# Adding three split products in one range of PSUM columns instead of two, in the first layer of a two-layer kernel

## The chip, the cores and the metric

The kernel runs on one core of a Trainium2 chip. The metric is the device time of one execution in microseconds (us), taken as the median over runs. TensorE (PE in the profile; its weight loads are listed apart as PEld) multiplies, VectorE is DVE, ScalarE is ACT, GpSimd is POOL, and SyncE (SP) issues the transfers.

## What is computed

The input x has 16 x 512 rows of 256 numbers. There are two layers, each the sum of x, an attention part and a feed-forward part, on a layernorm of x. In the first layer the attention part of the reference updates its weights from chunk to chunk, but what the kernel has to do for the output of this case is the gated product with the first weights, per head (4 heads of 64):

```python
x = L0_attn_hidden_states
xn = _layernorm(x, axis=-1)
# per head, q normalised:
gq = silu(W0 @ q);  hq = W2 @ q;  o = W1 @ (gq * hq)
# feed-forward part: top 2 of 16 experts by softmax, two shared experts
routed = jnp.einsum('bse,bseo->bso', g_topk, xe)
shared = (jnp.einsum('bsd,eod->bso', u, Ws) + jnp.sum(bs, axis=0)) / N_s
x = x + o + (xn + routed + shared)
xn = _layernorm(x, axis=-1)
x = x + attention(xn) + (xn @ w_ternary.T * alpha + bias)
```

The sequence is one chunk long (512), so the update of the weights touches no output. The product `o = W1 @ (gq * hq)` is the one that the change concerns.

## The kernel before

All matrices are held in two parts, a high part in the fp32r type and the rest (a low part), and a product is the sum of three: high by high, high by low, low by high. The helper `three` (L689 to L694) issues them one after the other into the same PSUM columns.

The first layer is `phase_a`. It handles 64 tiles of 128 rows, and every engine runs the same sequence of "slots" s, in which parts of several tiles are interleaved by hand: the layernorm of tile s+3, transposes and router of tile s+2, the normalised q of tile s+1, the experts of tile s, the sum of tile s-1 and the second layer's layernorm and ternary product of tile s-2. `for_slots` (L243) writes out the first slots and the last, and between them runs a loop of 14 iterations with four slots each.

On TensorE (`slot`, L728) a slot goes: experts pair 0, transposes of xn (L737), pair 1, [the hidden products in odd slots], pair 2, router (psR), pair 3, transposes of qn and gate (L763, L764), pair 4, transposes of xr (L775), pair 5, [the hidden products in even slots], pair 6, the ternary product (psT), then the base group of tile s-1 in psB, and pair 7. The 16 experts are worked in 8 pairs, each a group of 6 matmuls with 512 columns into one of the two banks of psM; a pair may start when the former user of its bank has been read, by ScalarE for pairs 1, 4 and 6 and by VectorE (`add_experts`, L525 and L528) for the others.

The base group (L792 to L814) is the place of the change. For each of the four heads it multiplies the hidden values `hd` (high and low, as the stationary operand) with `w1`, in which high and low part of a head lie side by side: w1[:, h, 0] and w1[:, h, 1], 64 columns each. L808 takes both as one moving operand of 128 columns and writes two ranges of psB at once, columns of the first 256 for high by high and of the second 256 for high by low. L809 adds low by high into the first range. Then `three` adds the shared experts and the biases into the first range, and `base_pe` is raised.

On VectorE (`slot`, L543) the sum of tile s-1 comes near the end of the slot: L671 adds the first range of psB to acc, L673 adds the second range, L676 adds GpSimd's sum accp and writes x1. `sum_dve` is raised by the first two, and by each wait on `sum_dve` VectorE waits for its own result; TensorE waits for it before it writes psB again (L801). Behind L676 come the two L528 of pair 7 (`add_experts(s, 7, 9)`), then in the next slot L548 (statistics of x) and pair 0 (L525, L528). GpSimd starts its sum of the tile after next with L339 once x1 is written (`x1_dve`).

Of the kernel before, what the change touches and what calls it, by code (L numbers as in the profile page):

```python
# [23 lines left out]
ALU = mybir.AluOpType  # L24
# [4 lines left out]
D = 256  # L29
# [32 lines left out]
def after(eng, sem, per, step, k):  # L62

    value = step.times(per, k)
    if step.reg is not None:
        assert step.scale * per + per * step.const + k > 0
        eng.wait_ge(sem, value)
    elif value > 0:
        eng.wait_ge(sem, value)
# [13 lines left out]
def phase_a(nc, io, xT_hi, xT_lo, base_dram, early):  # L83
# [3 lines left out]
    with ExitStack() as ctx:  # L87
        def sb(name, shape, dt=F32):
            return ctx.enter_context(nc.sbuf_tensor(f"{name}_a", shape, dt))
# [12 lines left out]
        w1 = sb("w1", [P, FH, 2, FD], F32R)  # L102
# [40 lines left out]
        acc = sb("acc", [P, 2, D])  # L143
# [12 lines left out]
        def bank(name, n=1):  # L156
            return ctx.enter_context(nc.psum_tensor(f"{name}_a", [P, n, 512], F32))

        psM = bank("psM", 2)
        psB = bank("psB")  # L160
# [37 lines left out]
        for q in range(NE * D // 2048):  # L198
            for k in range(KD):
                cols = slice(q * 2048, (q + 1) * 2048)  # L200
# [21 lines left out]
        def pair_of(n):  # L222

            return n.slot(4) // 2, n.const % 2
# [248 lines left out]
        def _(v):  # L473
# [69 lines left out]
            def slot(s):  # L543
# [9 lines left out]
                if bk.within(0, NT):  # L553
                    r = bk.slot(2)
# [12 lines left out]
                if bk.within(0, NT):  # L567
                    r = bk.slot(2)
                    v.bn_aggr(stats1[:, r, 6:8], stats1[:, r, 0:6]).then_inc(bk_dve, 1)
                if bk.within(0, NT):  # L570
                    r = bk.slot(2)
# [8 lines left out]
                if bk.within(0, NT):  # L580
                    r = bk.slot(2)
# [7 lines left out]
                if f1.within(0, NT):  # L589
                    r, q = f1.slot(2), f1.slot(4)  # L590
# [14 lines left out]
                if f2.within(0, NT):  # L605
                    r, t = pair_of(f2)
# [3 lines left out]
                if f1.within(0, NT):  # L610
                    r, q = f1.slot(2), f1.slot(4)
# [10 lines left out]
                if f2.within(0, NT):  # L622
                    r = f2.slot(4)
# [7 lines left out]
                if bk.within(0, NT):  # L631
                    r = bk.slot(2)
# [11 lines left out]
                if f1.within(0, NT):  # L644
                    r, q = f1.slot(2), f1.slot(4)
# [12 lines left out]
                if bk.within(0, NT):  # L658
                    r = bk.slot(2)
# [5 lines left out]
                last = s + -1  # L665
                if last.within(0, NT):

                    r = last.slot(2)
                    after(v, base_pe, 1, last, 1)
                    after(v, m_dve, 10, last, 10)  # L670
                    v.tensor_tensor(acc[:, r], psB[:, 0, 0:D], acc[:, r], ALU.add).then_inc(sum_dve, 1)  # L671
                    after(v, sum_dve, 2, last, 1)
                    v.tensor_tensor(acc[:, r], psB[:, 0, D:2 * D], acc[:, r], ALU.add).then_inc(sum_dve, 1)  # L673
                    after(v, m_pool, 7, last, 7)
                    after(v, sum_dve, 2, last, 2)
                    v.tensor_tensor(x1[:, r], acc[:, r], accp[:, r], ALU.add).then_inc(x1_dve, 1)  # L676
                if s.within(0, NT):
                    add_experts(s, 7, 9)
# [1 line left out]
                if s.reg is None:  # L680
                    if s.const == -3:
                        v.wait_ge(const_in, 16 * 4)
                    for c in SPLITS.get(s.const, ()):
                        split_low(c)
            for_slots(v, slot)

        @block.tensor
        def _(pe):
            def three(out, left, right, start, stop):  # L689

                (lh, ll), (rh, rl) = left, right
                pe.matmul(out, lh, rh, start=start, stop=False)  # L692
                pe.matmul(out, lh, rl, start=False, stop=False)  # L693
                return pe.matmul(out, ll, rh, start=False, stop=stop)  # L694
# [33 lines left out]
            def slot(s):  # L728
                f1, f2, bk = s + 2, s + 1, s + -2
                here = s.within(0, NT)  # L730
                if here:
                    experts(s, 0)
                if f1.within(0, NT):
                    after(pe, ln_dve, 3, f1, 3)
                    after(pe, ffn_dve, 1, s + -3, 1)
                    for k in range(KD):
                        mm = pe.transpose(psT[:, 0, k * P:(k + 1) * P], xn[:, f1.slot(4), k * P:(k + 1) * P], ident[:])  # L737
                    mm.then_inc(t1_pe, 1)
                if here:
                    experts(s, 1)  # L740
                    if s.const % 2 == 1:
                        hidden(s)
                    experts(s, 2)
                if f1.within(0, NT):
                    q = f1.slot(4)
                    if f1.reg is None and f1.const == 0:
                        pe.wait_ge(split_dve, SHARED)
                    after(pe, t1_dve, 1, f1, 1)
                    after(pe, r_dve, 9, f1 + -1, 3)
                    after(pe, r_act, 2, f1 + -1, 2)  # L750
                    for k in range(KD):
                        mm = three(psR[:, 0, 0:D + NE], (xt[0][:, q, k], xt[1][:, q, k]),
                                   (wq[0][:, k], wq[1][:, k]), k == 0, k == KD - 1)
                    mm.then_inc(r_pe, 1)
                if here:
                    experts(s, 3)
                if f2.within(0, NT):
                    r = f2.slot(2)
                    after(pe, qn_dve, 4, f2, 4)
                    after(pe, r_dve, 9, f2, 9)  # L760
                    after(pe, t2_dve, 2, f2 + -1, 2)
                    for p in range(FH // 2):
                        pe.transpose(psQ[:, 0, p * P:(p + 1) * P], qn[:, r, p * P:(p + 1) * P], ident[:])  # L763
                    pe.transpose(psQ[0:NG, 0, D:D + P], gate[:, f2.slot(4)], ident[:]).then_inc(t2_pe, 1)  # L764
                if here:
                    experts(s, 4)
                if bk.within(0, NT):
                    r = bk.slot(2)
                    after(pe, bk_dve, 6, bk, 6)
                    if f1.within(0, NT):  # L770
                        after(pe, t1_dve, 1, f1, 1)
                    else:
                        after(pe, ffn_dve, 1, bk + -1, 1)
                    for k in range(KD):
                        mm = pe.transpose(psT[:, 0, k * P:(k + 1) * P], xr[:, r, k * P:(k + 1) * P], ident[:])  # L775
                    mm.then_inc(t3_pe, 1)
                if here:
                    experts(s, 5)
                if s.const % 2 == 0:
                    hidden(s)  # L780
                if here:
                    experts(s, 6)
                if bk.within(0, NT):
                    r = bk.slot(2)
                    if bk.reg is None and bk.const == 0:
                        pe.wait_ge(split_dve, TERN + 1)
                    after(pe, t3_dve, 1, bk, 1)
                    for k in range(KD):
                        mm = three(psT[:, 0, 0:D], (xrt[0][:, r, k], xrt[1][:, r, k]),
                                   (wtern[0][:, k], wtern[1][:, k]), k == 0, k == KD - 1)  # L790
                    mm.then_inc(ffn_pe, 1)
                last = s + -1  # L792
                if last.within(0, NT):
                    q, (pair, t) = last.slot(4), pair_of(last)
                    after(pe, t2_dve, 2, last, 2)

                    after(pe, g_pool, 1, s if s.const % 2 == 1 else last, 1)
                    if last.reg is None and last.const == 0:
                        pe.wait_ge(split_dve, SHARED + 1)
                        pe.wait_ge(tern_dve, 4)  # L800
                    after(pe, sum_dve, 2, last + -1, 2)  # L801


                    out = psB[:, 0, :].rearrange("p (a n) -> p a n", a=2)
                    for h in range(FH):
                        hidden_h = [part[:, pair, h // 2, h % 2, t * P:(t + 1) * P] for part in hd]
                        cols = slice(h * FD, (h + 1) * FD)
                        pe.matmul(out[:, :, cols], hidden_h[0], w1[:, h], start=(h == 0), stop=False)  # L808
                        pe.matmul(out[:, 0, cols], hidden_h[1], w1[:, h, 0], start=False, stop=False)  # L809
                    for k in range(KD):  # L810
                        three(psB[:, 0, 0:D], (xt[0][:, q, k], xt[1][:, q, k]), (wshare[0][:, k], wshare[1][:, k]),
                              False, False)
                    mm = three(psB[:, 0, 0:D], (gt[0][:, q], gt[1][:, q]), (biases[0][:], biases[1][:]), False, True)
                    mm.then_inc(base_pe, 1)  # L814
                if here:
                    experts(s, 7)

                if s.reg is None and s.const == -1:

                    pe.wait_ge(tern_dve, 3)  # L820
                    pe.matmul(psB[:, 0, 0:1], ones[:], delta[:, 0:1], start=True, stop=True).then_inc(tern_pe, 1)

            for_slots(pe, slot)


# [636 lines left out]
```

## Time and profile before

| | us |
|---|---|
| median of 3 runs | 3497.76 |
| lowest and highest run | 3495.58, 3498.99 |
| span of the profiled execution | 3494.6 |
| TensorE busy | 3358.8 (96%) |
| TensorE weight loads busy | 2724.2 (78%) |
| VectorE busy | 2492.1 (71%) |
| GpSimd busy | 2364.7 (68%) |
| ScalarE busy | 1951.5 (56%) |

The span runs from the first to the last instruction of the profiled execution; the page gives no further time of that execution. The shares are means over both layers, so they are to be read again for the first layer alone, by a window. A matmul's duration in the records contains its way through the array, so that several overlap: what it costs in a row of matmuls is the distance between starts, not the duration. A wait is listed with the engine that ended it.

### The profile page before, as it was taken

The page shows a single profiled execution, that of the slowest core. Times are in us where ns is not written, and L with a number is a line of the kernel's source. Part 1 is how long each engine was busy: PE and PEld are TensorE (multiplying, and loading weights), DVE is VectorE, ACT ScalarE, POOL GpSimd, SP SyncE. Part 2 cuts the span into 40 slices and gives each one's busy share as a digit, 9 for nine tenths or more (in the row PEclk, how much of TensorE's full clock was granted, in tenths as well). Part 3 has the DMA queues.
Part 4 walks back from the last instruction along what each step waited for, and adds up shares of the span by engine and source line. Part 5 has one row for each costly group of instructions (what it writes and reads, how often), then busy time and mean ns, then how long its engine had stood idle before and what let it go on. Part 6 is the DMA issues. An engine that isn't in the chain of part 4 may idle for free.

```text
span 3494.6 us, 58322 instructions
## 1 busy us (share of the span) xinstructions
PE 3358.8 (96%) x16386; PEld 2724.2 (78%) x16386; DVE 2492.1 (71%) x4709; ACT 1951.5 (56%) x3226; POOL 2364.7 (68%) x2084
## 2 busy tenths in 40 slices
PE   5999999999999869999999999999999999999997
PEld 4877777777777757888888888888888888888886
DVE  6877877777778666666666666666667666666674
ACT  3333333333333247766767767667667667667774
POOL 4666666666666537777777777777777777777775
PEclk9999999999999979999999999999999999999998
DMA  2110001100110032222222222222222222222221
GB/s 78 31 31 29 27 29 30 31 27 28 31 30 28 26 96 61 51 65 70 46 70 56 62 72 51 65 73 49 67 70 46 70 56 59 70 53 68 70 48 47
DMA packets 195098, 180.22 MB, mean 52 GB/s; under 512 B 87954, under 2 KB 155812, under 8 KB 194468
## 3 DMA queue, kind: packets, MB, share of 16 engines
q1 hardware_dynamic: 194980, 179.04, 20.2%
q14 instruction: 92, 0.75, 0.1%
q8 instruction: 26, 0.43, 0.1%
HBM read 77.25 MB, written 34.08 MB: 32 GB/s over the span
## 4 chain that ended last, share of the span: by engine, by line
PE 61%; DMA 1%; DVE 1%; ACT 1%; POOL 1%; issue 0%; SPq 0%; POOLq 0%; ACTq 0%; DVEq 0%
PE psV_b L1342 7%; PE psV_b L1347 7%; PE psS_b L1330 7%; PE psS_b L1329 7%; PE psV_b L1343 7%; PE psN_b L1315 6%; PE psY_b L1270 3%; PE psY_b L1272 3%; PE psY_b L1271 3%; PE psX_b L1271 3%; PE psX_b L1272 3%; PE psX_b L1270 3%; PE psN_b L1399 2%; POOL pp_lo_b L1061 1%; DMA xT_lo<-xT_lo_dram 0%
## 5 line engine op out<-in xcount | busy, mean ns | idle before, releaser
L1061 POOL TENSOR_TENSOR pp_lo_b<-pf_b,pp_hi_b 128x1024 fp32r<-128x1024 f32 x512 | 1228.3, 2399 | 632.6 <-ACT pp_hi_b L1103 545.5
L1206 DVE TENSOR_REDUCE negmax_b<-psN_b 128x2 fp32r<-128x1024 f32 x512 | 627.1, 1225 | 387.1 <-PE psN_b L1315 379.2
L1098 ACT ACTIVATE pf_b<-psS_b 128x1024 f32<-128x1024 f32 x512 | 526.1, 1027 | 244.6 <-PE psS_b L1330 241.4
L692 PE MATMUL psM_a<-wr_hi_a,xt_hi_a 128*128 128x512 f32 x1024 | 440.2, 430 | 47.2 <-DVE acc_a L528 39.1
L1329 PE MATMUL psS_b<-qA_b,kA_b 128*128 128x512 f32 x1024 | 405.6, 396 | 5.6 <-DVE qB_b L1221 3.9
L694 PE MATMUL psM_a<-wr_hi_a,xt_lo_a 128*128 128x512 f32 x1024 | 409.9, 400 | 0.0
L693 PE MATMUL psM_a<-wr_lo_a,xt_hi_a 128*128 128x512 f32 x1024 | 407.8, 398 | 0.0
L1330 PE MATMUL psS_b<-qB_b,kB_b 68*128 68x512 f32 x1024 | 406.5, 397 | 0.0
L1342 PE MATMUL psV_b<-pp_hi_b,vals_hi_b 128*128 128x512 f32 x1024 | 402.5, 393 | 1.4
L1343 PE MATMUL psV_b<-pp_hi_b,vals_lo_b 128*128 128x512 f32 x1024 | 401.9, 392 | 0.0
L1315 PE MATMUL psN_b<-kA_b,qA_b 128*128 128x512 f32 x1024 | 323.2, 396 | 4.5 <-DVE negmax_b L1206 4.5
L1347 PE MATMUL psV_b<-pp_lo_b,vals_hi_b 128*128 128x512 f32 x1024 | 318.0, 392 | 4.6 <-POOL pp_lo_b L1061 4.5
L1122 ACT ACTIVATE kA_b<-psX_b 64x512 fp32r<-64x512 f32 x256 | 152.2, 595 | 302.7 <-PE psX_b L1272 297.9
L528 DVE SCALAR_TENSOR_TENSOR acc_a<-psM_a,gate_a,acc_a 128x256 f32<-128x256 f32 x576 | 277.2, 481 | 28.1 <-PE psM_a L694 16.5
L692 PEld LDWEIGHTS psM_a<-wr_hi_a,xt_hi_a 128*128 128x128 f32 x1024 | 194.6, 190 | 110.3 <-DVE acc_a L528 51.7
L1195 DVE SCALAR_TENSOR_TENSOR kB_b<-psX_b,kA_b 64x512 fp32r<-64x512 f32 x256 | 176.2, 688 | 141.2 <-ACT kA_b L1122 137.2
L1103 ACT ACTIVATE pp_hi_b<-pf_b 128x1024 fp32r<-128x1024 f32 x256 | 271.7, 1061 | 8.1
L409 ACT ACTIVATE scaled_a<-psM_a,gate_a 128x256 f32<-128x256 f32 x384 | 160.6, 469 | 184.2 <-PE psM_a L694 184.2
L1216 DVE CAST pp_hi_b<-pf_b 128x1024 fp32r<-128x1024 f32 x256 | 232.5, 908 | 5.1 <-ACT pf_b L1098 5.1
L1315 PEld LDWEIGHTS psN_b<-kA_b,qA_b 128*128 128x128 f32 x1024 | 193.7, 191 | 53.8 <-DVE negmax_b L1206 8.0
L1329 PEld LDWEIGHTS psS_b<-qA_b,kA_b 128*128 128x128 f32 x1024 | 193.6, 189 | 51.8 <-DVE qB_b L1221 6.5
L1342 PEld LDWEIGHTS psV_b<-pp_hi_b,vals_hi_b 128*128 128x128 f32 x1024 | 192.5, 188 | 50.8 <-DVE vals_lo_b L1238 7.4
(200 smaller groups left out, 7867.7 us busy)
## 6 DMA issues: line engine op xcount, KB each, us to landing
kA_b<-kA_b SPq DMA_DIRECT2D x128, 256.0 KB, 3.1
qB_b<-qA_b SPq DMA_DIRECT2D x128, 256.0 KB, 2.9
inverse_b<-inverse_dram SPq DMA_DIRECT2D x256, 128.0 KB, 3.0
x_a<-x_dram SPq DMA_DIRECT2D x64, 128.0 KB, 2.1
xT_hi_dram<-xrt_hi_a SPq DMA_DIRECT2D x64, 128.0 KB, 2.1
xT_lo_dram<-xrt_lo_a SPq DMA_DIRECT2D x64, 128.0 KB, 2.1
base_dram<-base_a SPq DMA_DIRECT2D x64, 128.0 KB, 1.8
xT_hi<-xT_hi_dram SPq DMA_DIRECT2D x16, 512.0 KB, 4.0
```

Source lines behind the costliest of these rows:

```text
L692: pe.matmul(out, lh, rh, start=start, stop=False)
L693: pe.matmul(out, lh, rl, start=False, stop=False)
L694: return pe.matmul(out, ll, rh, start=False, stop=stop)
L1061: pool.tensor_tensor(pp[1][:, c], pf[:, c], pp[0][:, c].bitcast(F32), ALU.subtract).then_inc(pl_pool, 1)
L1098: a.activation(pf[:, c], psS[:], ACT.Exp).then_inc(exp_act, 1)
L1206: v.tensor_reduce(negmax[:, n.slot(2), 2 * c:2 * c + 2], psN[:], AX.X, ALU.max, negate=True).then_inc(mx_dve, 1)
L1315: mm = pe.matmul(psN[:, t], qA[:, s, i * P:(i + 1) * P], kA[:, s], start=True, stop=True)
L1329: pe.matmul(psS[:, t], kA[:, s, keys], qA[:, s], start=True, stop=False)
L1330: mm = pe.matmul(psS[:, t], kB[:, s, keys], qB[:, s], start=False, stop=True)
L1342: pe.matmul(psV[:, g.slot(2)], values(0, h, i), pp[0][:, c, t], start=(i == 0), stop=False)
L1343: pe.matmul(psV[:, g.slot(2)], values(1, h, i), pp[0][:, c, t], start=False, stop=False)
L1347: mm = pe.matmul(psV[:, g.slot(2)], values(0, h, i), pp[1][:, c, t], start=False, stop=(i == TB - 1))
```

## The change

The three products with w1 of a head go into the same 64 columns, in the first 256 of psB: high by high, high by low, low by high, each a matmul of 64 columns. That is 12 matmuls a tile for 8. The second range of psB is not written any more, VectorE's second addition L673 goes, and `sum_dve` counts one a tile.

```diff
@@ -669,10 +669,8 @@
                     after(v, base_pe, 1, last, 1)
                     after(v, m_dve, 10, last, 10)
                     v.tensor_tensor(acc[:, r], psB[:, 0, 0:D], acc[:, r], ALU.add).then_inc(sum_dve, 1)
-                    after(v, sum_dve, 2, last, 1)
-                    v.tensor_tensor(acc[:, r], psB[:, 0, D:2 * D], acc[:, r], ALU.add).then_inc(sum_dve, 1)
                     after(v, m_pool, 7, last, 7)
-                    after(v, sum_dve, 2, last, 2)
+                    after(v, sum_dve, 1, last, 1)
                     v.tensor_tensor(x1[:, r], acc[:, r], accp[:, r], ALU.add).then_inc(x1_dve, 1)
@@ -798,15 +796,15 @@
-                    after(pe, sum_dve, 2, last + -1, 2)
-
-
-                    out = psB[:, 0, :].rearrange("p (a n) -> p a n", a=2)
+                    after(pe, sum_dve, 1, last + -1, 1)
+
+
                     for h in range(FH):
                         hidden_h = [part[:, pair, h // 2, h % 2, t * P:(t + 1) * P] for part in hd]
                         cols = slice(h * FD, (h + 1) * FD)
-                        pe.matmul(out[:, :, cols], hidden_h[0], w1[:, h], start=(h == 0), stop=False)
-                        pe.matmul(out[:, 0, cols], hidden_h[1], w1[:, h, 0], start=False, stop=False)
+                        pe.matmul(psB[:, 0, cols], hidden_h[0], w1[:, h, 0], start=(h == 0), stop=False)
+                        pe.matmul(psB[:, 0, cols], hidden_h[0], w1[:, h, 1], start=False, stop=False)
+                        pe.matmul(psB[:, 0, cols], hidden_h[1], w1[:, h, 0], start=False, stop=False)
```

## Rows read from the trace of the kernel before

**Rows 1.** The page's first part: busy us, share of the span, instructions of each engine.
```profile
PE 3358.8 (96%) x16386; PEld 2724.2 (78%) x16386; DVE 2492.1 (71%) x4709; ACT 1951.5 (56%) x3226; POOL 2364.7 (68%) x2084
```

**Rows 2.** Busy time by stretch: length, each engine's busy us (instructions), clock, DMA share, GB/s.
```profile
60.00:1200.00 1140.00, 1100.69 (x5983) 897.39 (x5982) 900.84 (x2653) 378.69 (x1118) 739.58 (x1237) 0.99 0.10 28
1300.00:3400.00 2100.00, 2095.67 (x9721) 1700.18 (x9720) 1457.28 (x1830) 1469.76 (x1955) 1524.93 (x733) 1.00 0.25 61
```

**Rows 3.** Waits of PE, 183 to 1140 us: us in total, times, longest.
```profile
PE psM_a L692 <- DVE acc_a L528: 37.1, 32, 2.2
```

**Rows 4.** Waits of DVE, 183 to 1140 us.
```profile
DVE acc_a L671 <- PE psB_a L694: 44.9, 52, 1.1
DVE stats_a L548 <- issue: 33.3, 13, 2.7
DVE acc_a L528 <- PE psM_a L694: 11.4, 52, 0.3
```

**Rows 5.** PEld in order of time (start us, us, instruction), base group of one tile.
```profile
601.90 0.19 PEld L808 LDWEIGHTS psB_a<-w_a,hd_hi_a 128*128 128x128 f32 x1
602.02 0.19 PEld L809 LDWEIGHTS psB_a<-w_a,hd_lo_a 128*128 128x128 f32 x1
...
602.80 0.19 PEld L692 LDWEIGHTS psB_a<-wshare_hi_a,xt_hi_a 128*128 128x128 f32 x1
602.91 0.19 PEld L693 LDWEIGHTS psB_a<-wshare_lo_a,xt_hi_a 128*128 128x128 f32 x1
...
603.71 0.18 PEld L692 LDWEIGHTS psB_a<-biases_hi_a,gt_hi_a 18*128 18x128 f32 x1
603.82 0.18 PEld L693 LDWEIGHTS psB_a<-biases_lo_a,gt_hi_a 18*128 18x128 f32 x1
```

**Rows 6.** PE in order of time, products with 256 columns of the next tile.
```profile
618.69 0.28 PE L692 MATMUL psT_a<-wtern_hi_a,xrt_hi_a 128*128 128x256 f32 x1
618.81 0.28 PE L693 MATMUL psT_a<-wtern_lo_a,xrt_hi_a 128*128 128x256 f32 x1
```

**Rows 7.** PE in order of time, w1 products of that tile.
```profile
619.54 0.31 PE L808 MATMUL psB_a<-w_a,hd_hi_a 128*128 128x128 f32 x1
619.68 0.24 PE L809 MATMUL psB_a<-w_a,hd_lo_a 128*128 128x64 f32 x1
619.76 0.31 PE L808 MATMUL psB_a<-w_a,hd_hi_a 128*128 128x128 f32 x1
```

**Rows 8.** DVE in order of time, end of one slot, with idle time and releaser.
```profile
604.46 0.42 DVE L671 TENSOR_TENSOR acc_a<-psB_a,acc_a 128x256 f32<-128x256 f32 x1 [1.06 <-PE psB_a L694]
604.92 0.42 DVE L673 TENSOR_TENSOR acc_a<-psB_a,acc_a 128x256 f32<-128x256 f32 x1
605.45 0.42 DVE L676 TENSOR_TENSOR x_a<-acc_a,accp_a 128x256 f32<-128x256 f32 x1
606.07 1.00 DVE L528 SCALAR_TENSOR_TENSOR acc_a<-psM_a,gate_a,acc_a 128x256 f32<-128x256 f32 x2 [0.20 <-PE psM_a L694]
606.99 0.42 DVE L548 BATCH_NORM_STATS2 stats_a<-x_a 128x6 f32<-128x256 f32 x1
```

**Rows 9.** DVE, then PE, in order of time at a boundary of the loop.
```profile
476.49 1.00 DVE L528 SCALAR_TENSOR_TENSOR acc_a<-psM_a,gate_a,acc_a 128x256 f32<-128x256 f32 x2 [0.19 <-PE psM_a L694]
480.01 0.43 DVE L548 BATCH_NORM_STATS2 stats_a<-x_a 128x6 f32<-128x256 f32 x1 [2.52 <-issue]
...
478.99 0.40 PE L694 MATMUL psM_a<-wr_hi_a,xt_lo_a 128*128 128x512 f32 x1
481.40 0.50 PE L692 MATMUL psM_a<-wr_hi_a,xt_hi_a 128*128 128x512 f32 x1 [2.01 <-DVE acc_a L528]
```

**Rows 10.** In order of time, after the last tile's base group.
```profile
1219.55 0.42 DVE L673 TENSOR_TENSOR acc_a<-psB_a,acc_a 128x256 f32<-128x256 f32 x1
...
1224.92 0.69 PE L775 MATMUL psT_a<-ident_a,xr_a 128*128 128x128 f32 x2 [5.86 <-DVE xr_a L588]
```

**Rows 11.** Busy time of two loop iterations, columns as in rows 2.
```profile
477.10:550.80 73.70, 71.23 (x385) 58.19 (x384) 58.09 (x173) 24.39 (x72) 47.61 (x81) 0.98 0.10 29
550.80:624.10 73.30, 70.14 (x387) 57.05 (x386) 58.26 (x173) 24.25 (x72) 47.73 (x81) 1.00 0.10 29
```

## The prediction

> **What bounds the kernel now.** I read the page's busy shares first: TensorE is busy 96% of the span, VectorE 71% [rows 1]. Then the busy times cut by stage, since the change touches the first layer only (all of it ends before about 1230 us). In the first layer TensorE is busy 1100.69 of 1140 us and VectorE 900.84; in the second, 2095.67 of 2100 [rows 2]. The printed chain that ended last names lines of the second layer only, so for the first I read waits instead. In the steady part (183 to 1140 us, 52 tiles) TensorE waited for other engines in one place only: 37.1 us in 32 waits for VectorE's L528, which frees a bank of psM [rows 3]. So the first layer goes at TensorE's pace, with some 4% of waits for VectorE in it. VectorE for its part waited for TensorE ahead of every L671 (44.9 us in 52 waits) and ahead of the L528 that follows L676 (11.4 us in 52 waits), and lost 33.3 us at L548 to "issue", 13 times [rows 4]. The reader is to see here that VectorE is late only at certain points, and to ask of each saving whether it lies between the last release by TensorE and such a point.
>
> **Part 1, the products with w1 on TensorE (terms that decide).** Before, a tile has 8 of them: four with 128 moving columns (L808) and four with 64 (L809). After, twelve with 64. The moving columns are the same, 4 x 128 + 4 x 64 = 768 and 12 x 64 = 768. What grows is the number of weight loads, 8 to 12, as each matmul here has a load of its own. In the trace the eight loads begin at 601.90 and the load that follows them at 602.80: 0.90 us for eight, 0.1125 us each, and the spacing is the same behind a product with 128 columns as behind one with 64 [rows 5]. The load of the biases, 18 rows high, is also followed by the next after 0.11 us [rows 5], and products with 256 columns, twice the work of L808, start 0.12 us apart [rows 6]. So up to 256 columns the price of a product is the price of its load, nearly whatever the columns are. Twelve then take 12 x 0.1125 = 1.35 us, 0.45 more than now. The trace has no run of products of 64 columns alone. Its bounds are 0.11 us (the nearest load spacing) and 0.12 us (256 columns): 4 x 0.11 to 4 x 0.12 = 0.44 to 0.48 us. I take 0.45, since the eight loads are the same loads of the same tiles. There are 64 tiles (16 x 512 rows by 128), and the group is issued by the engine that sets the pace, behind no wait: 64 x 0.45 = 28.8 us (28.2 to 30.7).
>
> The matmul starts alone can be read otherwise: 0.14 us from an L808 to its L809 and 0.08 from that to the next L808 [rows 7], as if time went by columns. The Trainium skill, "TensorE: Matmul & The Clock Gate", section "Back-to-back issue gap", gives a table of that kind: about 60 cycles for 1 to 64 columns and 134 for 128. By it alone, at 2.4 GHz, eight products would take 4 x 56 + 4 x 25 = 324 ns and twelve 300 ns (an estimate from that page), and the change would cost nothing here. Its section "LDWEIGHTS (loading the stationary operand)" says instead that a load takes its columns over 1.2, 107 ns for 128; the trace's 0.11 us agrees with this and not with the table, so the sum stands as it was made from rows. The column reading is the first rival below.
>
> **Part 2, the order of additions in the same columns.** Each of the 64 columns of a head is now written three times, about 0.11 us apart; now the L809 adds to columns that L808 wrote 0.14 us before, and in the products with 256 columns the same place is added to after 0.12 us without a hold [rows 6, 7]. I cost it at nothing; the price if it held is a rival.
>
> **Part 3, VectorE's second addition.** L673 goes, with its wait. L671 to L676 start 604.46, 604.92 and 605.45; the next L528 starts at 606.07, with 0.20 us of idle time that ended with TensorE's psM [rows 8]. Without L673, L676 starts 0.53 us earlier by the row starts, but not the L528: it waits for TensorE's pair 7, which now comes after a base group that is 0.45 us longer. So relative to TensorE the L528 starts when it did, and all that follows it on VectorE too. Its idle time grows from 0.2 to some 0.7 us; that 0.5 us is spent in front of a release that TensorE gives. Fifty-two of 52 tiles show this wait [rows 4].
>
> Does the saving reach TensorE's waits by another way? The large wait is at a loop boundary, once in four tiles: L528 twice at 476.49, then nothing until L548 at 480.01 ("issue", 2.52 us), then L525 and L528, and only then TensorE's next product, idle 2.01 us until 481.40 [rows 9]. That delay starts at the end of the L528s, hence at TensorE's pair 7. The smaller waits (32 less 13 loop boundaries, 19 in all; 37.1 - 13 x 2.0 = 11 us) come later in the slot, at experts(s, 5) behind the transposes of L775, and hang on the same sequence. The base group lies ahead of pair 7 and behind both waits, so its extra 0.45 us covers neither. GpSimd's L339, released by L676, comes 0.5 us earlier relative to TensorE, and with it the load of x; neither ends a wait of TensorE. I cost the whole of part 3 at nothing, except at the end: after the last tile's base group there is no pair 7, and the way goes L671, L673, L676 ... to L775 at 1224.92 and on to the second layer [rows 10]. There it gives back 0.5 us, once. The changed wait on sum_dve in TensorE (one count a tile for two) was long satisfied and stays so.
>
> **Part 4, the clock.** Loop iterations of four tiles alternate between 73.70 us at a mean granted clock of 0.98 and 73.30 us at 1.00 [rows 11]: a stretch at the lower level (1.2 GHz) behind the loop boundary's wait costs 0.4 us. The wait stays, and the iterations get 1.8 us longer, so which of them get it can change: between none and all of 14, against half now, it is 7 x 0.4 = 2.8 us either way. I take none and keep it for the range. Nothing of the second layer changes but its start.
>
> **The sum.** 28.8 - 0.5 = 28.3 us. On the profiled span, 3494.6 us, this gives 3522.9. The page gives no time around the span; the median of the runs, 3497.76 us, lies 3.2 us above the span, and I carry this over: 3497.8 + 28.3 = 3526.1, say 3526.0 (+0.8%).
>
> **The rivals.**
> - Time goes by columns (the case on the other side, not slower): a load of 0.08 us or less would let twelve products take 12 x 0.08 = 0.96 us, 0.06 more than the 0.90 now, 64 x 0.06 = 3.8 us less 0.5: 3501. The point from which it decides is a load spacing under 0.08 us. For it: the 0.14/0.08 pattern of starts [rows 7]. Against it: the even 0.11 us of loads, the 18-row loads, and 256 columns at 0.12 [rows 5, 6]. The same time results if the change doesn't do what it says, because the second product with the same left operand needs no load. Against that: L692 and L693 of every `three` have the same left operand, and L693 has its load [rows 5]. Together 6%.
> - VectorE's saving reaches TensorE in each of the 32 waits: 32 x 0.5 = 16 us off, 3510. It would need L528 of pair 7 to wait for L676 and not for TensorE. For it: the slack is only 0.2 us [rows 8], and 0.6 us of TensorE's idle time or more stands behind it. Against: TensorE's part gets longer, so the slack only grows. 5%.
> - Additions into the same columns hold each other up: if a product had to wait for the end of the one before (0.24 us of duration against 0.11 of spacing [rows 7]), eight of twelve would cost 0.13 us more, 1.04 us a tile, 67 us: 3593. 3%.
> - Forecast: loads set the price, VectorE's saving becomes waiting. 86%.
>
> **How the numbers follow.** The forecast's own range: the low side is 28.2 us of loads, 0.5 at the end, 2.8 for the clock and 2 for the spread of the runs (3495.58 to 3498.99), some 3520; the high side 30.7 and half of the clock's 2.8, 3530. With a little of the second rival I give 3519 to 3532. Outside stand the first rival, the third and most of the second, 14%. A measurement of this kernel tells a change from none at about 0.2%, 7 us. Slower by more: forecast, second and third rival, 0.93 in all, with what may lie between them left aside. Within 0.2%: the first rival, 0.06. Faster: both first and second rival at once, 0.01.
>
> **What would show it.** In the profile after, twelve loads of the w1 products should span about 1.35 us, 0.11 apart, and the tile slot of 17.4 us should become 17.85 (18.4 where it was 17.95); four tiles together 75.1 to 75.5 for 73.3 to 73.7. VectorE's wait for TensorE ahead of the pair 7 L528 should grow from 0.2 to about 0.7 us, and that ahead of L671 from 0.9 to 1.3. TensorE's waits for L528 should stay at some 37 us in the steady part. The prediction is wrong if the loads come closer than 0.1 us, if the L528 is no longer released by psM, or if TensorE's 37 us shrink by ten or more.

## The result, and the profile after

The changed kernel takes 3524.5 us (median of 4 runs, 3523.1 to 3528.1) against 3498.1 for the kernel before, a ratio of 1.0076 (95% interval 1.0062 to 1.0091): 26.4 us slower. The profiled span is 3523.0 us.

The page's first part, after: TensorE has 256 matmuls and 256 loads more (4 for each of 64 tiles), VectorE 64 instructions less and 31 us less work, and the time went up all the same. It answers to rows 1.

```profile
PE 3382.8 (96%) x16642; PEld 2747.9 (78%) x16642; DVE 2460.9 (70%) x4645; ACT 1948.2 (55%) x3226; POOL 2361.5 (67%) x2084
```

The weight loads in order of time, one tile's base group after (start us, busy us). The line numbers are two lower from L674 on; L805 to L807 are the three products, and L690 begins the shared experts. It answers to rows 5.

```profile
614.37 0.19 PEld L805 LDWEIGHTS psB_a<-w_a,hd_hi_a 128*128 128x128 f32 x1
614.49 0.19 PEld L806 LDWEIGHTS psB_a<-w_a,hd_hi_a 128*128 128x128 f32 x1
614.60 0.19 PEld L807 LDWEIGHTS psB_a<-w_a,hd_lo_a 128*128 128x128 f32 x1
...
615.72 0.19 PEld L690 LDWEIGHTS psB_a<-wshare_hi_a,xt_hi_a 128*128 128x128 f32 x1
```

From 614.37 to 615.72 are 1.35 us for twelve loads, and the first two of them load the same operand, each for itself. The end of a slot on VectorE, after; it answers to rows 8.

```profile
617.38 0.42 DVE L671 TENSOR_TENSOR acc_a<-psB_a,acc_a 128x256 f32<-128x256 f32 x1 [1.50 <-PE psB_a L692]
617.91 0.42 DVE L674 TENSOR_TENSOR x_a<-acc_a,accp_a 128x256 f32<-128x256 f32 x1
618.99 1.00 DVE L528 SCALAR_TENSOR_TENSOR acc_a<-psM_a,gate_a,acc_a 128x256 f32<-128x256 f32 x2 [0.66 <-PE psM_a L692]
```

The L528 waits 0.66 us for 0.20: the addition's time is there, as idle time in front of TensorE's psM. The waits of the steady part, 183 to 1164 us, TensorE's and then two of VectorE's (us in total, times, longest); they answer to rows 3 and 4.

```profile
PE psM_a L690 <- DVE acc_a L528: 40.0, 36, 2.2
...
DVE acc_a L671 <- PE psB_a L692: 73.2, 53, 1.8
...
DVE acc_a L528 <- PE psM_a L692: 35.8, 54, 0.7
```

The windows don't hold the same number of waits. TensorE waits for VectorE hardly longer than before (40.0 us in 36 waits for 37.1 in 32), and not less, though VectorE has half a microsecond a tile less to do; what grew is VectorE's own waiting for TensorE: ahead of L671 from 0.86 us a tile (44.9 in 52) to 1.38 (73.2 in 53), ahead of L528 from 0.22 (11.4 in 52) to 0.66 (35.8 in 54).

Where the time went, by the first and the last base group (the view of one line: durations min/median/max in ns, first and last start in us, number of starts), of before and of after:

```profile
L808 PEld LDWEIGHTS psB_a<-w_a,hd_hi_a x256: 187/192/333, 71.7 to 1216.0; 128*128 128x128 f32 x128
```

```profile
L805 PEld LDWEIGHTS psB_a<-w_a,hd_hi_a x256: 187/192/333, 71.7 to 1242.6; 128*128 128x128 f32 x128
```

The stretch from one to the other grew from 1144.3 to 1170.9 us, by 26.6 us. The last of these starts is the fourth head's, so the stretch holds 63 whole groups and three loads more than before in the last: 63 x 0.45 + 3 x 0.11 = 28.7 us by the loads alone.

### The profile page after: what moved, and what is told of

It reads as the page before. It is cut to its first block, busy times and chain, and to the rows that moved or that the text cites. A ratio compares the mean times of both kernels' runs of the same rounds, so it can differ in the third digit from the quotient of the medians.

```text
span 3523.0 us, 58742 instructions
## 1 busy us (share of the span) xinstructions
PE 3382.8 (96%) x16642; PEld 2747.9 (78%) x16642; DVE 2460.9 (70%) x4645; ACT 1948.2 (55%) x3226; POOL 2361.5 (67%) x2084
## 4 chain that ended last, share of the span: by engine, by line
PE 61%; ACT 1%; DVE 1%; DMA 1%; POOL 1%; issue 0%; SPq 0%; POOLq 0%; ACTq 0%; DVEq 0%
PE psV_b L1340 7%; PE psV_b L1345 7%; PE psS_b L1328 6%; PE psV_b L1341 6%; PE psS_b L1327 6%; PE psN_b L1313 6%; PE psY_b L1268 3%; PE psY_b L1270 3%; PE psY_b L1269 3%; PE psX_b L1269 3%; PE psX_b L1270 3%; PE psX_b L1268 3%; PE psN_b L1397 2%; POOL pp_lo_b L1059 0%; DVE vals_lo_b L1236 0%
## 5 line engine op out<-in xcount | busy, mean ns | idle before, releaser
L690 PE MATMUL psM_a<-wr_hi_a,xt_hi_a 128*128 128x512 f32 x1024 | 438.8, 428 | 50.1 <-DVE acc_a L528 42.0
L692 PE MATMUL psM_a<-wr_hi_a,xt_lo_a 128*128 128x512 f32 x1024 | 408.2, 399 | 0.0
L1345 PE MATMUL psV_b<-pp_lo_b,vals_hi_b 128*128 128x512 f32 x1024 | 318.1, 392 | 4.6 <-POOL pp_lo_b L1059 4.4
L528 DVE SCALAR_TENSOR_TENSOR acc_a<-psM_a,gate_a,acc_a 128x256 f32<-128x256 f32 x576 | 277.0, 481 | 56.7 <-PE psM_a L692 45.1
L690 PEld LDWEIGHTS psM_a<-wr_hi_a,xt_hi_a 128*128 128x128 f32 x1024 | 193.3, 189 | 114.0 <-DVE acc_a L528 55.6
```

What stands on the lines that cost most here:

```text
L1345: mm = pe.matmul(psV[:, g.slot(2)], values(0, h, i), pp[1][:, c, t], start=False, stop=(i == TB - 1))
```

## The experiments

Every time stands beside runs of the kernel before on the same chip. The kernel before had a median of 3498.8 us beside the first four, 3497.4 beside the next four and 3495.6 beside the last two. Where two experiments are compared, it is by their medians. The code cuts show the lines that matter, against the kernel before or the changed one; the counts in the waits on `sum_dve` change with them and are left out.

**VectorE's half of the change alone.** TensorE as before, L673 gone (against the kernel before).

```diff
                     v.tensor_tensor(acc[:, r], psB[:, 0, 0:D], acc[:, r], ALU.add).then_inc(sum_dve, 1)
-                    after(v, sum_dve, 2, last, 1)
-                    v.tensor_tensor(acc[:, r], psB[:, 0, D:2 * D], acc[:, r], ALU.add).then_inc(sum_dve, 1)
```

> Left out: the high-by-low product of w1 is still computed but not added (L673 goes), so x1 lacks it. TensorE's eight products stay as before. My theory: the 0.5 us that VectorE saves a tile turns into waiting for pair 7 of psM, so the time is that of the kernel before less 0.5 us at the end (3497.5, ratio 1.000); VectorE's idle time ahead of the L528 that follows L676 grows from 0.2 to 0.7 us. Rival (the saving reaches TensorE's 32 waits): 16 us less, 3482, ratio 0.995.

Measured: 3498.2 us, ratio 1.000 (0.9991 to 1.0009). VectorE's end of a slot in this kernel:

```profile
587.70 0.43 DVE L674 TENSOR_TENSOR x_a<-acc_a,accp_a 128x256 f32<-128x256 f32 x1
588.77 1.00 DVE L528 SCALAR_TENSOR_TENSOR acc_a<-psM_a,gate_a,acc_a 128x256 f32<-128x256 f32 x2 [0.64 <-PE psM_a L692]
```

64 additions of 0.42 us can go from the second busiest engine and the time stays. The rival's 16 us are outside the interval (0.9991 is 3 us).

**TensorE's half alone.** Against the changed kernel: this is the changed kernel with an addition of the same shape put back.

```diff
                     v.tensor_tensor(acc[:, r], psB[:, 0, 0:D], acc[:, r], ALU.add).then_inc(sum_dve, 1)
+                    after(v, sum_dve, 2, last, 1)
+                    v.tensor_tensor(acc[:, r], psB[:, 0, 0:D], acc[:, r], ALU.add).then_inc(sum_dve, 1)
```

> Changed in the computation: the changed kernel with psB's range added to acc a second time by VectorE, an addition of the same shape as the one that went; x1 gets it twice. My theory: as the changed kernel, or 0.5 us more (3525, ratio to the kernel before 1.008), since the addition fits into VectorE's wait, which has 0.7 us. Rival (the missing addition had given something back): up to 16 us more, 3541, ratio 1.012.

Measured: 3526.0 us, ratio 1.0079 (1.0065 to 1.0093). The two halves taken apart give nothing and the whole. With the addition back the L528 waits 0.20 us again:

```profile
618.42 1.00 DVE L528 SCALAR_TENSOR_TENSOR acc_a<-psM_a,gate_a,acc_a 128x256 f32<-128x256 f32 x2 [0.20 <-PE psM_a L694]
```

**Columns or loads: eight products of 64 columns.** Against the kernel before; L673 is gone too.

```diff
-                        pe.matmul(out[:, :, cols], hidden_h[0], w1[:, h], start=(h == 0), stop=False)
-                        pe.matmul(out[:, 0, cols], hidden_h[1], w1[:, h, 0], start=False, stop=False)
+                        pe.matmul(psB[:, 0, cols], hidden_h[0], w1[:, h, 0], start=(h == 0), stop=False)
+                        pe.matmul(psB[:, 0, cols], hidden_h[1], w1[:, h, 0], start=False, stop=False)
```

> Left out: the high-by-low product of w1. As e1_no_second_add, but L808 has 64 moving columns for 128, so eight products of 64 columns a tile. My theory (a load sets the price): the time of e1, within 2 us; eight loads 0.11 us apart. Rival (time goes by columns): four products of 0.08 us for 0.14, so 0.24 us a tile less, 64 x 0.24 = 15 us less than e1.

Measured: 3498.3 us, 0.1 us from e1_no_second_add. A third of the moving columns (768 to 512 a tile) went and gave nothing. Its loads start 0.11 us apart from 584.13 on, as before:

```profile
584.13 0.19 PEld L806 LDWEIGHTS psB_a<-w_a,hd_lo_a 128*128 128x128 f32 x1
584.24 0.19 PEld L805 LDWEIGHTS psB_a<-w_a,hd_hi_a 128*128 128x128 f32 x1
```

**Columns or loads: twelve products of 128 columns.** Against the changed kernel, as the next three.

```diff
-                        pe.matmul(psB[:, 0, cols], hidden_h[0], w1[:, h, 0], start=(h == 0), stop=False)
-                        pe.matmul(psB[:, 0, cols], hidden_h[0], w1[:, h, 1], start=False, stop=False)
-                        pe.matmul(psB[:, 0, cols], hidden_h[1], w1[:, h, 0], start=False, stop=False)
+                        out = psB[:, 0, :].rearrange("p (a n) -> p a n", a=2)[:, :, cols]
+                        pe.matmul(out, hidden_h[0], w1[:, h], start=(h == 0), stop=False)
+                        pe.matmul(out, hidden_h[0], w1[:, h], start=False, stop=False)
+                        pe.matmul(out, hidden_h[1], w1[:, h], start=False, stop=False)
```

> Changed in the computation: all twelve products have 128 moving columns (high and low part of w1 together) and write both ranges of psB; the first range gets high by high twice and lacks high by low, the second is never read. My theory: the time of the changed kernel within 2 us (3525), for 128 columns still fit under a load. Rival (columns, 0.14 us for 128): 12 x 0.14 = 1.68 us a tile for 1.35, 21 us more, 3546.

Measured: 3523.7 us, ratio 1.0080 (1.0063 to 1.0097), as the changed kernel, which has half the columns. With e3_eight_of_64 this is a square of two by two: eight products of 64 columns or of 64 and 128 (e1_no_second_add) 3498, twelve of 64 or of 128 columns 3524. The number of products sets the time, their width doesn't.

**The load's price by itself.** The left operand of the twelve products cut to 64 of the tile's 128 rows; the three lines of the changed kernel's products that these replace are left out, and so is the flag by which the shared experts now start the sum in the first range.

```diff
+                        half = [x[:, 0:P // 2] for x in hidden_h]
+                        out = psB[0:P // 2, 0, D + h * FD:D + (h + 1) * FD]
+                        pe.matmul(out, half[0], w1[:, h, 0], start=(h == 0), stop=False)
+                        pe.matmul(out, half[0], w1[:, h, 1], start=False, stop=False)
+                        pe.matmul(out, half[1], w1[:, h, 0], start=False, stop=(h == FH - 1))
```

> Left out: the three products with w1 don't reach x1, and are computed for half of the rows only: the twelve products have a left operand of 64 rows of the tile instead of 128 (64 columns in the load) and write the second range of psB, which is not read. It measures the price of a load by its columns. My theory: a load of 64 columns lets the next follow after 0.06 us or little more, so twelve take 0.7 to 0.9 us for 1.35, and the time is 29 to 42 us below the changed kernel, 3483 to 3496. Rival (a product has a price of 0.11 us whatever the load): 3525 as the changed kernel.

Measured: 3485.9 us, ratio 0.9971 (0.9959 to 0.9982), 38.6 us below the changed kernel's 3524.5. The loads of one group in order of time:

```profile
579.91 0.13 PEld L808 LDWEIGHTS psB_a<-w_a,hd_hi_a 128*64 128x64 f32 x1
579.97 0.14 PEld L809 LDWEIGHTS psB_a<-w_a,hd_lo_a 128*64 128x64 f32 x1
580.03 0.14 PEld L807 LDWEIGHTS psB_a<-w_a,hd_hi_a 128*64 128x64 f32 x1
...
580.55 0.19 PEld L690 LDWEIGHTS psB_a<-wshare_hi_a,xt_hi_a 128*128 128x128 f32 x1
```

They follow each other after 0.06 us, and the group (579.79 to 580.55) takes 0.76 us for 1.35: 64 x 0.59 = 37.8 us, within 1 us of the difference measured. So the 0.11 us go with the columns of the load; a product of 64 moving columns (here with half the rows in its output) takes 0.06 us or less and was hidden. The edit halves the load and the rows of the output together, and no run parts the two.

**More of the same.** A fourth product a head, low by low.

```diff
                         pe.matmul(psB[:, 0, cols], hidden_h[1], w1[:, h, 0], start=False, stop=False)
+                        pe.matmul(psB[:, 0, cols], hidden_h[1], w1[:, h, 1], start=False, stop=False)
```

> The changed kernel with a fourth product a head, low by low, into the same 64 columns: 16 products of 64 columns a tile for 12. My theory (load price 0.11 us each, linear): 64 x 0.45 = 28 us more than the changed kernel again, 3553, ratio to the kernel before 1.016. Rival (columns, 0.08 us each): 20 us more, 3545. Rival (the changed kernel's cost is something that comes once, such as waits): no more than 3530.

Measured: 3561.0 us, ratio 1.0183 (1.0169 to 1.0197): 36.4 us above the changed kernel where 28 were expected. The group's own price was right: its loads start at 610.99, the load behind them at 612.78, 1.79 us, 0.44 more than with twelve. The other 8 us are not in it. The busy times by loop iteration (length, each engine's busy us, granted clock, DMA share, GB/s) show three of the thirteen:

```profile
422.00:499.10 77.10, 73.63 (x418) 60.57 (x416) 56.18 (x169) 24.18 (x72) 47.69 (x80) 1.00 0.09 28
499.10:576.40 77.30, 74.83 (x417) 61.80 (x416) 56.29 (x169) 24.33 (x72) 47.69 (x80) 0.98 0.09 28
...
964.30:1042.60 78.30, 75.47 (x419) 62.01 (x418) 56.16 (x169) 24.19 (x72) 47.68 (x80) 0.98 0.09 27
```

Nine of thirteen iterations have a stretch at 1.2 GHz here (a mean granted clock of 0.98 in the row), against three in the changed kernel. And where it falls into a slot with no wait at a loop boundary, as in the second row below, the slot takes 20.42 us, where the same kind of slot elsewhere in this kernel takes 18.85 (the first row; both from base group to base group), 1.6 us more instead of 0.4.

```profile
610.99:629.84 18.85, 18.38 (x106) 15.17 (x105) 14.30 (x45) 5.36 (x19) 11.55 (x21) 1.00 0.12 35
...
998.26:1018.68 20.42, 19.92 (x107) 16.32 (x106) 14.35 (x45) 5.37 (x19) 11.53 (x21) 0.92 0.11 33
```

The whole first layer has ten such stretches ahead of its end. Three fall into slots without the boundary's wait, one of them ahead of the loop (1.6 us each); two fall into a boundary's slot but ahead of its wait (22.5 us where such slots take some 21.5 without one: 1.0 each); five lie behind the wait (21.9 to 22.0 us: 0.4 to 0.5 each). Together these are 9 us, and the changed kernel's three, all behind the wait, cost 1.6: the difference accounts for 7 of the 8 us. Why they fall more often with 16 products was not tried.

**The same columns three times in a row.** The twelve products ordered by kind, so that four heads lie between two additions to the same columns.

```diff
-                    for h in range(FH):
+                    for left, right in ((0, 0), (0, 1), (1, 0)):
+                        for h in range(FH):
```

> The changed kernel with its twelve products in another order: high by high of all four heads, then high by low, then low by high, so that the same columns are written again after four products and not at once. My theory: the time of the changed kernel within 2 us (additions into the same columns hold nothing up). Rival (they do): part of the 28 us comes back.

Measured: 3524.8 us, ratio 1.0079 (1.0062 to 1.0096). Adding at once to the same place, 0.11 us after the product before, costs nothing that these runs can tell.

**The wait at the loop boundary.** The kernel before with eight slots in an iteration (the block number in the addresses of SyncE's transfers is adapted to it, which the cut leaves out).

```diff
-                with eng.Fori(1, B - 1) as it:
-                    for j in range(TB):
-                        slot(Step(it, TB, j))
+                with eng.Fori(1, B // 2) as it:
+                    for j in range(2 * TB):
+                        slot(Step(it, 2 * TB, j - TB))
```

> The kernel before with the first layer's loop written out for eight slots an iteration: 7 iterations for 14, nothing else. It tests what the wait of 2.0 us at a loop boundary is worth, behind which the saved addition could not show. My theory: each boundary costs TensorE 2.0 us, and with its clock stretch 0.4 more in half of them; seven boundaries less give 14 to 17 us, less some 0.65 each where the wait of the ordinary slot (17.95 for 17.4) takes its place, so 9 to 15 us less than before, 3483 to 3489. Rival: VectorE's pause comes from fetching instructions and comes as often with a longer loop: 3498.

Measured: 3477.2 us, ratio 0.9948 (0.9932 to 0.9965): 20 us less, more than I expected. VectorE's waits in the steady part:

```profile
DVE stats_a L549 <- issue: 15.0, 6, 2.6
```

It was 33.3 us in 13 times [rows 4]: the pause comes once a jump back, whatever lies between. A boundary is worth 20.3 / 7 = 2.9 us, more than the 2.0 of the row, which is why my sum of 9 to 15 was short. The kernel before shows where the rest is. TensorE's two waits in one boundary slot, then that slot (546.08 on) and another with a stretch at 1.2 GHz behind the wait, both from base group to base group:

```profile
555.11 0.50 PE L692 MATMUL psM_a<-wr_hi_a,xt_hi_a 128*128 128x512 f32 x1 [1.98 <-DVE acc_a L528]
...
561.61 0.50 PE L692 MATMUL psM_a<-wr_hi_a,xt_hi_a 128*128 128x512 f32 x1 [0.71 <-DVE acc_a L528]
```

```profile
546.08:566.55 20.47, 17.77 (x99) 14.19 (x97) 14.35 (x45) 5.38 (x19) 11.48 (x20) 1.00 0.11 33
472.36:493.35 20.99, 18.98 (x98) 15.39 (x97) 14.82 (x46) 5.51 (x19) 11.47 (x20) 0.92 0.11 32
```

In the kernel without a loop, which comes next, the slot of the same tile as the second of these takes

```profile
461.11:479.09 17.98, 17.49 (x99) 14.27 (x98) 14.63 (x46) 5.38 (x19) 11.40 (x20) 1.00 0.14 37
```

The wait of the ordinary slot is in the boundary's slot already (0.71 us for 0.5), and nothing takes the boundary's place, so the 0.65 us that I took off had no ground. A boundary costs 2.5 us, and 3.0 with the stretch at 1.2 GHz. With eight slots an iteration the profile has six boundaries for 13 and two stretches for seven: 7 x 2.5 + 5 x 0.5 = 20 us, which is what was measured.

**No loop at all**, in the kernel before and in the changed one.

```diff
-            if B > 2:
-                with eng.Fori(1, B - 1) as it:
-                    for j in range(TB):
-                        slot(Step(it, TB, j))
+            for s in range(TB, TB * (B - 1)):
+                slot(Step(None, TB, s))
```

> The kernel before with the first layer's 56 looped slots written out, no loop left. Theory after the loop of eight: VectorE's pause of 2.5 us belongs to the jump back, so the seven boundaries still left in the loop of eight go too and give the same 20 us again: 3457, ratio 0.989. Rival (long straight code has to be fetched with pauses of its own): 3477 or more, as with the loop of eight.

> The changed kernel with the same slots written out. It asks whether VectorE's saved addition is worth something once the wait at the loop boundary is gone. My theory: no, the change costs the same 28 us, less the clock's share: 3457 + 28 = 3485. Rival (the saving shows in the waits of the ordinary slot): 10 or more us less than that, 3475.

Measured: 3466.3 us for the kernel before without its loop, ratio 0.9917 (0.9900 to 0.9933), and 3495.6 for the changed kernel without it, ratio 0.9998 (0.9989 to 1.0008). The difference, 29.2 us, is the price of the change with the large wait gone; the saved addition is worth nothing there either. TensorE's waits (60 to 1200 us) in the first of the two:

```profile
PE psM_a L690 <- DVE acc_a L526: 15.0, 30, 0.7
```

What is left of the waits for psM are those of the ordinary slot, 0.5 us each. (The same view has 13.1 us in four waits for psT at the layer's end; the kernel before has the same four, the longest of them in rows 10.) The loop's second half gave 10.8 us more, not 20. Part of this is my miscount: six boundaries were left, not seven, and in the first layer they are worth what they should be, for the last base group starts at 1180.5 us, 15.5 us earlier than with the loop of eight (1196.0) and 35.5 earlier than before (1216.0). The rest is given back in the second layer. The last L1347 of the kernel before (L1345 here) starts at 3436.9 us for 3465.7, only 28.8 us earlier, which is near the 29.2 of the medians; some 6.6 us of the lead are gone. (The span is 32.5 us shorter, as in the last 35 us of this execution the granted clock was 0.90, for 0.68 in that of the kernel before.) In the second layer, between 1500 and 3300 us, its weight loads have a wait that the kernel before doesn't show:

```profile
PEld psS_b L1327 <- ACT pf_b L1096: 8.1, 13, 0.8
```

Thirteen are as many as loop boundaries of the second layer in this stretch, whose code was not touched. Why ScalarE is later there was not found out, and that this wait is the 6.6 us is argued from its size only. Still, the kernel before without its loop is the fastest of all here, 29 us below the kernel before.

## Why the prediction was right, and where it was loose

**Loads set the price (part 1).** Right, and the deciding term. Predicted 0.45 us a tile from the load spacing, measured 1.35 less 0.90 (the tile slots of 17.4 and 17.95 us became 17.84 and 18.40, for 17.85 and 18.4 in the prediction); e3_eight_of_64 and e4_twelve_of_128 show that width doesn't count up to 128 columns, e7_short_loads that the price halves with the columns of the load. What misled in rows 7, matmuls 0.14 and 0.08 us apart, was not time spent on columns: with products all of 64 columns the same eight take the same 0.90 us. The starts of matmuls shift within the beat of the loads; the beat has to be read from the loads. By the table of the Trainium skill, "TensorE: Matmul & The Clock Gate", section "Back-to-back issue gap", taken alone as in the prediction, the change would have cost nothing (an estimate from that page). It should not have been taken alone: the section gives the table for an isolated product and says that in a stream of load and product pairs both set the spacing, which is what these runs show. Its figure for such a stream, about 81 ns with 128 columns, was not met here: the spacing was 0.11 us. The section "LDWEIGHTS (loading the stationary operand)", columns over 1.2, gives 107 and 53 ns for 128 and 64 columns (an estimate from that page), and the traces show 0.11 and 0.06 us.

**Order of additions (part 2).** Right at nothing: e6_other_columns_between (3524.8 us for 3524.5).

**VectorE's addition (part 3).** Right. The idle time ahead of the L528 grew from 0.20 to 0.66 us (predicted 0.7), TensorE's wait did not shrink (37.1 and 40.0 us), and e1_no_second_add shows the saving to be worth nothing even without TensorE's new work. The 0.5 us given back after the last tile is there in the trace (TensorE waits 5.40 us ahead of the transposes of xr, for 5.86 in rows 10) but too small to be told in the medians.

**The clock (part 4).** I put this term at zero and kept 2.8 us either way for the range. The trace has fewer stretches at 1.2 GHz. Two iterations of the changed kernel, without and with one (columns as in rows 2):

```profile
487.30:562.30 75.00, 71.84 (x402) 58.83 (x401) 56.22 (x169) 24.22 (x72) 47.70 (x80) 1.00 0.10 29
787.30:862.90 75.60, 73.16 (x402) 60.04 (x401) 56.42 (x169) 24.36 (x72) 47.64 (x80) 0.98 0.10 28
```

Seven of thirteen iterations had one before, three of thirteen now: 4 x 0.4 to 0.6 = 1.6 to 2.4 us given back. Thirteen iterations took 956.3 us and now 977.5: 21.2 more, where 52 x 0.45 = 23.4 were to be expected and the clock's 2 us are the rest. At the second layer's first product the two kernels are 26.4 us apart (1238.5 and 1264.9).

That this is also the difference of the medians is partly luck. The profiled spans, 3494.6 and 3523.0, are 28.4 us apart: in these two executions the second layer, whose code is the same, took 2.0 us more, and no cause was found. The other runs say that the clock does count. The 17 recorded executions with twelve products of 128-column loads (this kernel, e2, e4, e6) have a median granted clock of 0.989, the 44 of the kernel before that ran beside the experiments 0.986. At an equal clock they are about 30 us apart: 3526.9 (mean of 3) and 3497.0 (of 10) at 0.987, 3524.9 (of 5) and 3494.4 (of 7) at 0.988. By this comparison the change costs about 30 us, somewhat more than its loads, and the clock gives some 3 to 4 of it back. Why the full clock is granted more often is not shown.

**The rivals.** Time by columns: excluded by e3, e4 and the result. A second product with the same left operand without a load: excluded by the loads of L805 and L806, 0.12 us apart. The saving reaching TensorE: excluded by e1 (3498.2 for 3482). Additions holding each other up: excluded by e6 and by the loads' even 0.11 us.

## What to carry to other kernels

Where the left operand changes with every product and a product has few columns, count weight loads and not columns: packing high and low part of a narrow right operand into one product cost nothing here at 128 columns beside a load of 128, and splitting it cost a load each time, 0.11 us. Wider products were not tried in this place; elsewhere in the kernel before, those with 256 columns start 0.12 us apart [rows 6] and those with 512 (psM) 0.23 us, so the columns outlast the load somewhere from 256 on. Before work is moved from one engine to another, look for the release that ends the idle time behind the saved instruction: if the engine that got the new work gives it, the saving is only waiting. A wait that comes once a loop iteration may belong to the jump back and not to any work; a longer loop body makes it rarer. Count all that the wait drags behind it (here 2.5 to 3.0 us for a wait of 2.0), and look at the stages behind for what is given back.

## What the runs showed of the hardware that I had not expected

- In this program two products with the same left operand back to back (L692 and L693 of a `three`, L805 and L806 of the changed kernel) load it twice, 0.11 to 0.12 us each; the second load is not saved.
- VectorE's jump back costs a pause of 2.5 us each time, independent of the body's length (13 times, 33.3 us in all, with four slots; 6 times, 15.0 us, with eight; none without a loop), and a boundary cost 2.5 us of the first layer, 3.0 with a stretch at 1.2 GHz behind its wait.
- Writing out the first layer's loop gained 35.5 us there and 29.2 us of the whole; the second layer, whose code is the same, became slower.
- Sixteen narrow products a tile for twelve brought more stretches at 1.2 GHz (nine of thirteen iterations for three), which cost 0.4 to 0.5 us behind the boundary's wait, 1.0 ahead of it and 1.6 us in a slot without one: 7 of the 8 us beyond the price of the loads.
